# Output stages of layers 0 and 1: the residual on GpSimd, three tokens on VectorE, the moments a tile later

## The reference

```python
xn = layer_norm(x, norm_w, norm_b)
left = lin(left_w, left_b) * sigmoid(lin(lgate_w, lgate_b))
right = lin(right_w, right_b) * sigmoid(lin(rgate_w, rgate_b))
out_gate = sigmoid(lin(ogate_w, ogate_b))
out = einsum('bkjd,bkid->bijd', left, right)
out = layer_norm(out, ton_w, ton_b)
out = einsum('bijh,dh->bijd', out, out_w) + out_b
return out * out_gate
```

## Time and profile before

| | us |
|---|---|
| median of 3 runs | 1699.05 |
| lowest and highest | 1698.02, 1703.9 |
| the profiled execution's own time | 1702.15 |
| its span in the trace | 1700.3 |
| busy in the span: TensorE, VectorE, ScalarE, GpSimd | 1274.0, 1346.3, 1079.1, 861.2 |

### The profile page before, as it was taken

One profiled execution on the slowest core, in us unless ns is written; L12 is line 12 of the kernel. 1 busy time (PEld: TensorE's weight loads), 2 busy tenths in 40 slices (PEclk: granted clock), 3 DMA queues, 4 the chain that ended last, 5 costly groups with the idle time before them and its releaser, 6 DMA issues.

```text
span 1700.3 us, 30071 instructions
## 1 busy us (share of the span) xinstructions
PE 1274.0 (75%) x9576; PEld 757.2 (45%) x9576; DVE 1346.3 (79%) x3955; ACT 1079.1 (63%) x2680; POOL 861.2 (51%) x591
## 2 busy tenths in 40 slices
PE   0488878976588878985999466676666477778899
PEld 0233367644233367553776133333333233337665
DVE  6787833998878725988999899999999677771497
ACT  0488823874688814973343577777775388871498
POOL 0799801541999602542555034444445787840264
PEclk9999998997799998987999669899998799998999
DMA  7244452775455363984443144444445344426387
GB/s 267 75 120 117 99 144 81 234 240 158 93 119 121 90 159 86 268 225 127 108 108 87 21 95 100 102 115 108 100 107 125 98 100 106 106 67 152 105 306 264
DMA packets 408781, 225.48 MB, mean 133 GB/s; under 512 B 343408, under 2 KB 343728, under 8 KB 408624
## 3 DMA queue, kind: packets, MB, share of 16 engines
q1 hardware_dynamic: 270192, 185.81, 39.8%
q10 hardware_dynamic: 138432, 37.76, 9.5%
HBM read 114.97 MB, written 66.06 MB: 106 GB/s over the span
## 4 chain that ended last, share of the span: by engine, by line
issue 27%; DVE 27%; POOL 21%; PE 15%; ACT 7%; DMA 2%; SPq 0%; POOLq 0%; DVEq 0%; ACTq 0%
POOL ln_s L516 7%; DVE stats L809 6%; PE ps L1347 5%; PE ps L1344 5%; POOL work L508 5%; ACT work L1105 5%; POOL work L522 4%; POOL work L486 3%; PE ps L1257 3%; DVE work L661 2%; DVE pairs L872 2%; POOL pairs L553 2%; ACT work L1119 2%; DVE stats L898 2%; DVE pairs L945 1%
## 5 line engine op out<-in xcount | busy, mean ns | idle before, releaser
L516 POOL TENSOR_TENSOR ln_s<-ln_s,half_power 128x8 f32<-128x8 f32 x216 | 356.0, 1649 | 420.6 <-DVE ln_s L818 364.9
L1270 PE MATMUL ps<-wfold,work 64*128 64x320 f32 x1728 | 339.5, 483 | 101.6 <-DVE pairs L872 53.2
L1105 ACT ACTIVATE work<-work,ln_s 128x64 f32<-128x64 f32 x576 | 212.4, 430 | 128.9 <-DVE ln_s L824 128.9
L1270 PEld LDWEIGHTS ps<-wfold,work 64*128 64x128 f32 x1728 | 136.7, 187 | 272.8 <-DVE pairs L872 133.3
L1107 ACT ACTIVATE work<-pairs,ln_s 128x64 f32<-128x64 f32 x756 | 233.3, 391 | 26.9 <-POOL ln_s L516 26.9
L872 DVE TENSOR_TENSOR pairs<-ps,work 128x256 f32<-128x256 f32 x288 | 169.0, 597 | 63.5 <-ACT work L1119 58.6
L1119 ACT ACTIVATE work<-ps 128x384 f32<-128x384 f32 x432 | 194.5, 476 | 4.9 <-PE ps L1270 3.8
L1086 ACT ACTIVATE work<-ps 128x512 f32<-128x512 f32 x216 | 128.0, 593 | 83.3 <-PE ps L1257 83.3
L1257 PE MATMUL ps<-ident,work 128*128 128x128 f32 x864 | 145.2, 294 | 43.7 <-ACT work L1105 29.8
L1166 ACT ACTIVATE pairs<-pairs,rescale 128x256 f32<-128x256 f32 x288 | 122.5, 498 | 70.0 <-DVE work L1003 70.0
L1347 PEld LDWEIGHTS ps<-work 128*128 128x128 f32 x864 | 113.5, 205 | 91.4 <-ACT work L1086 78.6
(11 more groups left out here) (163 smaller groups left out, 2448.7 us busy)
## 6 DMA issues: line engine op xcount, KB each, us to landing
work<-x_mid SPq DMA_DIRECT2D x144, 256.0 KB, 2.9
gate_dram<-work ACTq DMA_DIRECT2D x108, 256.0 KB, 2.8
work<-gate_dram SPq DMA_DIRECT2D x108, 256.0 KB, 3.9
work<-in_x_in SPq DMA_DIRECT2D x72, 256.0 KB, 2.9
work<-x_nat SPq DMA_DIRECT2D x144, 128.0 KB, 3.0
pairs<-in_x_in SPq DMA_DIRECT2D x4, 2304.0 KB, 19.0
work<-pairs SPq DMA_DIRECT2D x96, 96.0 KB, 3.1
work<-pairs ACTq DMA_DIRECT2D x96, 96.0 KB, 3.2
```

Source lines behind the costliest of these rows:

```text
L516: pool.tensor_tensor(ln_s[:, b, RSTD, :], ln_s[:, b, VAR, :], half_power[:, 0:U], ALU.pow)\
L1105: last = act.activation(to, normed[:, r, u * C:(u + 1) * C], ACT.Identity, scale=rstd, bias=ln_s[:, b, SHIFT, u:u + 1])
L1270: last = pe.matmul(ps[:, PAIR_BANKS[n % 3] + odd, 0:PROJ], xnT[rows, b, pair * P:(pair + 1) * P], wfold[rows, q, 0:PROJ], start=True, stop ...
```

## The change

The residual of layers 0 and 1 goes from VectorE to GpSimd, behind the power of the same iteration. VectorE normalises three tokens in these stages in place of one, ScalarE five in place of seven. The moments (and the bias folds) are called one tile later, since the new tile now comes from another engine. Layer 3 keeps its residual on VectorE.

```diff
-DVE_TOKENS = {(0, 0): 3, (0, 1): 1, (1, 0): 3, (1, 1): 1, (2, 0): 1, (3, 0): 2, (3, 1): 1}
+DVE_TOKENS = {(0, 0): 3, (0, 1): 3, (1, 0): 3, (1, 1): 3, (2, 0): 1, (3, 0): 2, (3, 1): 1}
...
+            def update_kept(l, t, b, r):
+
+                pool.wait_ge(prod_ready, x_base(l) + t + 1)
+                pool.wait_ge(res_loaded[r], tile_landed(RES_LOADS, l, t, r, RING))
+                if t >= KEPT:
+                    pool.wait_ge(xnew_stored[b], tile_landed(X_STORES, l, t - KEPT, b))
+                    pool.wait_ge(in_moments, sum(len(PARTS[k]) for k in range(l + 1)) + (t - KEPT) // 9 + 1)
+                pool.tensor_tensor(new_tile(l, t), gate[:, r, :], xres[:, r, :], ALU.add).then_inc(xnew_ready, 1)
...
-                    pipeline(pool, [(4, lambda t, b: token_rstd(l, 1, t, b))])
+                    updates = [(0, lambda t, b, r: update_kept(l, t, b, r), RING)] if l < 2 else []
+                    pipeline(pool, [(4, lambda t, b: token_rstd(l, 1, t, b)), *updates])
...
-                ahead = KEPT if l < 2 else 2
-                if t >= ahead:
-                    dve.wait_ge(xnew_stored[b], tile_landed(X_STORES, l, t - ahead, b))
+                if t >= 2:
+                    dve.wait_ge(xnew_stored[b], tile_landed(X_STORES, l, t - 2, b))
...
-                                                                (0, lambda t, b, r: update(l, t, b, r), RING),
-                                                                (0, lambda t, b: beside_update(l, t))]))
+                                                                *([(0, lambda t, b, r: update(l, t, b, r), RING)] if l == LAST else []),
+                                                                (-1, lambda t, b: beside_update(l, t))]))
```

## The result

The changed kernel took 1707.42 us in the median of 18 runs (1703.18 to 1720.09), the kernel before 1702.78 us beside it on the same chip (18 runs, 1697.0 to 1725.68). The ratio is 1.0039, 95% interval [1.0021, 1.0058]: 0.39% slower, within the half per cent called no difference, though the interval leaves out 1. The ratio is taken from runs within 1.5% of a kernel's fastest; of the 36 only the one of 1725.68 us lies outside. The profiled execution's own time is 1706.87 us, its span 1705.0.

The account below looks back on a forecast made before the run. VectorE was taken to bound full output-stage tiles at 3.21 us, replaced by a 3.00 us loop over VectorE and GpSimd. Layer 0 +1.6 and layer 1 -0.75 gave +0.9, forecast 1700.0 us, range 1693 to 1710.

Parts of the forecast that it names:

- the clock: Output stages: tiles at TensorE's lower clock cost 4.86 us, count kept; rival, 12% each way: 1697 or 1708 us.
- The loop of 3.00 us: Output-stage tiles: GpSimd's power and add, then VectorE's variance waiting for the add: 3.00 us, replacing 3.21 and 2.58.
- The light tiles of 2.58: Tiles without moments (before tile 9) took 2.58 us, set by ScalarE and TensorE; forecast 3.00 after, +0.42 each.
- The adds at 1.27: The residual add on GpSimd in the output stages was taken to last 1.27 us.
- add at its MLP median: Rival, 7%: GpSimd's add lasts 2.18 us as in the MLP, loop 3.91, +39 us, 1739.
- The fold tiles: Layer 0's two tiles with a bias fold: the fold waits for the add, 4.5 us where 3.64 before.
- The pause: Between tiles 23 and 24, where loads start anew: the later add delays stores and loads, +1.6 us a layer.
- Interval 24: From tile 24's gated product to the next: set by TensorE's lower clock, so 0 change.
- Intervals 30 to 34: End of each output stage, between gated products of tiles 30 to 35: 14.27 to 11.6 us, -2.6.
- The rival's −3.3: Clock rival's fast side, 12%: behind layer 0's pause two intervals of 4.86 become 3.00 and 3.39, 1697 us.
- No mutual waiting: Rival, 10%: variance and fold slip past the add; light tiles 2.83, full 2.97, fold tiles 3.37; 1694 us.
- the power holds the pair: Rival, 2%: GpSimd's power also locks the shared ports, loop 5.4 us, +2.2 for some 50 tiles, about 1810.

Follow-up runs that it names:

- the repeat: The changed kernel measured again with nothing altered: 1709.24 us, ratio 1.003 to the kernel before.
- Experiment 1: Changed kernel with the output stages' four BN_STATS writing to a free PSUM bank, so the variance reads PSUM: 1700.34 us, ratio 1.0002 to the kernel before.
- experiment 2: Changed kernel with one token instead of three on VectorE in the output stages of layers 0 and 1: 1710.03 us, ratio 1.0042 to the kernel before.
- experiment 5: Changed kernel with tile 23's residual added on VectorE behind its three tokens: 1706.29 us, ratio 1.0024 to the kernel before.
- experiment 9: Changed kernel with PSUM statistics, residuals of tiles 0 to 8, 23, 24 on VectorE, one token there to tile 11, then two: 1694.3 us, ratio 0.9954.

## Why the prediction was right, and where it was off

The forecast was no difference, 1700.0 us against 1699.05: a ratio of 1.0006. Measured is 1.0039, and 1.003 in the repeat. The class is right, the median lies in the range, and the mechanism was found in the right place; the forecast's +0.9 us is below the interval's lower end, 0.21% or 3.6 us. The total is right in part by luck: misses of both signs are in it, and in these two profiles the clock's terms cancel.

- **The loop of 3.00 us** holds for light and full tiles, to 0.02. Experiment 1 shows the handover as its cause in light tiles, experiment 2 that it gives 3.00 in full tiles too where VectorE has less to do. In full tiles of the changed kernel VectorE's own work, forecast at 2.97, measured 3.00 and would have given the same interval alone; the forecast gave the loop credit that it shares. The light tiles of 2.58 were put down to ScalarE and TensorE; by experiment 1 they are TensorE's.
- **The adds at 1.27** were right, all 72; the rival "add at its MLP median" (2.18) falls with them.
- **The fold tiles**: 4.36 for 4.5. The wait ends where it was put; the statistics behind the fold start 0.08 before it ends, and the sum had them one after the other.
- **The pause**: +1.4 for +1.6 in layer 0, +2.5 in layer 1 of this profile. By the means over all profiles it is +1.2 and +1.4: the mechanism (the add behind the power delays the stores, and the loads behind them) is shown by experiment 5, and the rest of layer 1's +2.5 is how late the gate lands, 6.1 us of waiting here and 5.5 in the repeat.
- **Interval 24 failed.** The forecast had TensorE's low clock decide in 24 to 26 and put 0. The rows say otherwise: 24 and 25 were VectorE's own 3.2 before, at the low clock too, and 26 waited 0.8 for TensorE; 25 and 26 gain 0.2 to 0.3 each, and 24 to 26 together lose 0.3 and 0.4. VectorE's tokens wait for an add that has no power in front of it: +0.8 a layer, shown by experiment 9. The text had applied the lock to the variance and the fold and had not asked where else an add could stand in front of a one-input VectorE instruction, though rows of the kernel before show one (59.73 above). L842's form above 0.3 us was on its own list of what would show it wrong, and came (1.32 at most).
- **Intervals 30 to 34 failed in size**: 12.65 for 11.6. Two of 2.42 were taken from VectorE's rows alone; GpSimd, late by then, runs two adds in a row, and interval 32 takes 3.46.
- **The clock**: the sum kept the tiles of 4.86 as they were. They moved from one place to another, −2.1 and −3.3 in layer 0, and in layer 1 +1.6 at intervals 0 and 1 and some +3.9 in 2 to 8, and nearly cancel. The rival's −3.3 behind layer 0's pause is what this profile has; the start of a stage, where layer 1 lost most, it did not name. The number of such tiles differs between two profiles of the same program, so the difference of one pair of profiles is not a property of the change.
- **No mutual waiting** and **the power holds the pair** fall: the variance waits up to 1.03 us for the add, and three tokens inside a power keep 0.65.

With the terms as measured (24 to 26 +0.7 for both layers, 30 to 34 +2.0, pauses by their means −0.6, folds −0.3, end −0.3) the forecast's +0.9 becomes about +2.4. The measured ratio is +6.6 us, with an interval from 3.6 to 9.9, so this is still below it. The profile's own sum over the two stages, +3.8, has the clock's terms nearly cancelling and pauses of +3.9 where the means give +2.6; without that excess it is the same +2.4. What makes up the other 4 us is not settled by these runs. Tiles at the lower clock vary enough from profile to profile to be it, but that the changed kernel has more of them on average is not shown.

## What to carry to other kernels

Moving work from a busy engine to an idle one is worth what the handover leaves. Before moving an operation to GpSimd, go through every VectorE instruction that can stand beside it in time, in light tiles, at folds, behind pauses and at the end, and not in the typical tile alone. Keep the operation on VectorE in tiles where VectorE has slack and where the next load waits for it, and let a small instruction read PSUM instead of SBUF if it must run beside a GpSimd add; all of it together made of a change that costs 0.4% one that gains 0.5%, while the pause alone (experiment 5) moved the time by less than could be resolved. When a tile has three limits within 5% of each other, an edit that takes one away can leave its time as it was, as in experiments 1 and 2; the wait inside the instruction shows the effect, the interval does not.

## What the runs showed of the hardware

- The wait reaches VectorE instructions with a single SBUF tensor input. A tensor_scalar of 128x64 took up to 1.32 us beside an add (0.27 alone), one of 128x8 up to 1.03 (0.17 alone). A scalar_tensor_tensor with two such inputs took 1.53 (0.56 alone). With its source in PSUM the 128x8 one kept 0.165 to 0.167 in all 72 cases. The Trainium skill (VectorE: DVE Perf Modes, "Why PSUM operands drop a tier") says that the mode which takes both SBUF read ports is closed to PSUM operands; the 72 durations agree with that.
- The statistics' BN_STATS (L819) kept 0.26 to 0.30 us, and the gated product with one input in PSUM 0.66 to 0.69, in all tiles of the changed kernel, beside adds or not.
- GpSimd's power of 128x8 lasts 1.64 us and holds nobody back: three tokens inside it take 0.65 us, an add of 128x512 with both inputs in SBUF 0.67 (experiment 5, 370.17). Read by the Trainium skill (SBUF — State Buffer, "SBUF: two separate sides") a GpSimd instruction would hold the pair for its whole length. The add does in these rows; the power does not.
- An add on GpSimd that starts after a token has started does stop the following ones: at 376.67 and 376.84 above the tokens were first by 0.17 us and still took 1.68 for three.
